# Two fp16 parts for the probabilities, second masks on TensorE, the projection a round later

## The reference, cut to what matters

```
def _layer(x, wqkv, qs, ksc, wo, lg, lb, w1, b1, w2, b2):
    h = shift_token(x)                         # second half of the columns from the row before
    q, k, v = split(h @ wqkv)                  # 8 heads of 64
    q, k = rotary_xpos(l2norm(q) * qs, l2norm(k) * ksc)
    # windows of 128: each query sees its own and the previous window,
    # masked to i >= j and i <= j + 128
    o = softmax(8 * q @ k.T, masked) @ v
    x = x + o @ wo
    h = layernorm(shift_token(x)) * lg + lb    # eps 1e-5
    a, g = split(h @ w1 + b1)                  # 682 columns each
    return x + (a * gelu(g)) @ w2 + b2
```

## Time and profile before

| | |
|---|---|
| median of three runs | 3973.07 us (3972.77 to 3973.07) |
| the profiled execution's own time | 3974.68 us |
| its span | 3972.9 us |
| mean granted clock of TensorE | 0.960 of its upper level |
| busy: TensorE, its weight loads | 3510.6 us, 2099.6 us |
| busy: VectorE, ScalarE, GpSimd | 2638.4, 2148.6, 1522.5 us |
| DMA | 139 MB, 35 GB/s in the mean |

### The profile page before, as it was taken

The page is one execution under the profiler, slowest core; times in us unless marked ns, Lnnn a source line. Parts: engine busy times, 40 slices in busy tenths (PEclk is TensorE's granted clock), DMA queues, the critical chain, the costliest instruction groups (busy, mean ns, idle before and its releaser), DMA issues.

```text
span 3972.9 us, 72434 instructions
## 1 busy us (share of the span) xinstructions
PE 3510.6 (88%) x26976; PEld 2099.6 (53%) x26976; DVE 2638.4 (66%) x4180; ACT 2148.6 (54%) x2585; POOL 1522.5 (38%) x1584
## 2 busy tenths in 40 slices
PE   2888888888866799999999999887999999999999
PEld 1223232323224566667666766555666766667666
DVE  4778777777744567666676666656677666776664
ACT  0566565656543356555555555443655556555554
POOL 1212121111114345455455554343455544455443
PEclk7999999999987899999999999998999999999999
DMA  2222222222120000010000101010000110001101
GB/s 56 48 60 54 58 55 57 56 56 57 45 82 6 14 21 19 18 34 19 21 18 18 34 19 42 20 50 19 27 24 24 34 35 25 24 27 31 37 19 35
DMA packets 149003, 139.02 MB, mean 35 GB/s; under 512 B 11132, under 2 KB 147376, under 8 KB 148912
## 3 DMA queue, kind: packets, MB, share of 16 engines
q1 hardware_dynamic: 148912, 137.78, 13.1%
HBM read 70.40 MB, written 33.55 MB: 26 GB/s over the span
## 4 chain that ended last, share of the span: by engine, by line
issue 29%; POOL 21%; PE 15%; DVE 4%; ACT 2%; POOLq 0%; DMA 0%; SPq 0%; DVEq 0%; ACTq 0%
POOL f_u L1478 7%; POOL f_u L1483 5%; PE f_p L1104 3%; PE f_p L1123 3%; POOL f_hT L1494 3%; POOL f_Pl L1502 2%; PE f_p L1145 2%; PE f_p L1023 2%; POOL f_xb L1511 2%; PE f_p L1086 2%; POOL f_Pl L1504 1%; POOL f_qst L1488 1%; PE f_p L1090 1%; POOL f_mark_l L1499 1%; DVE f_negm L1360 1%
## 5 line engine op out<-in xcount | busy, mean ns | idle before, releaser
L654 DVE TENSOR_REDUCE m_negm<-m_p 128x2 f16<-128x1024 f32 x512 | 608.3, 1221 | 170.4 <-PE m_p L473 168.5
L576 ACT ACTIVATE m_Pr<-m_p 128x1024 f32<-128x1024 f32 x512 | 500.6, 1020 | 163.9 <-PE m_p L492 159.4
L1478 POOL TENSOR_TENSOR f_u<-f_u,f_bt 128x1024 f32<-128x1024 f32 x128 | 301.9, 2358 | 561.2 <-DVE f_bt L1332 561.2
L1104 PE MATMUL f_p<-f_vl,f_Pl 128*128 128x65 f32 x3584 | 426.1, 279 | 30.7 <-POOL f_Pl L1504 30.7
L1104 PEld LDWEIGHTS f_p<-f_vl,f_Pl 128*128 128x128 f32 x3584 | 416.0, 195 | 41.0 <-POOL f_Pl L1504 31.4
L1229 ACT ACTIVATE f_Pl<-f_p 128x896 f32<-128x896 f32 x256 | 220.5, 914 | 328.8 <-PE f_p L1090 221.6
L1494 POOL TENSOR_TENSOR f_hT<-f_gates,f_hT 128x512 f16<-128x512 f32 x192 | 223.8, 1166 | 396.5 <-ACT f_gates L1252 395.1
L501 PE MATMUL m_o<-m_Pr,m_vm 128*32 128x512 f32 x2048 | 341.6, 645 | 13.0 <-ACT m_Pr L576 13.0
L1023 PE MATMUL f_p<-f_wq_h,f_xT_h 128*128 128x512 f16 x768 | 295.8, 385 | 62.4 <-DVE f_mark_x L1318 45.1
L1244 ACT ACTIVATE f_gates<-f_p,f_bias 128x512 f32<-128x512 f32 x192 | 131.4, 684 | 344.8 <-PE f_p L1145 344.7
L1360 DVE TENSOR_REDUCE f_negm<-f_p 128x4 bf16<-128x1024 f32 x256 | 295.7, 1222 | 15.0 <-PE f_p L1056 15.0
(11 more groups left out here) (219 smaller groups left out, 7533.7 us busy)
## 6 DMA issues: line engine op xcount, KB each, us to landing
f_xs<-out SPq DMA_DIRECT2D x32, 512.0 KB, 4.8
f_xr<-out SPq DMA_DIRECT2D x32, 512.0 KB, 4.6
out<-f_xb SPq DMA_DIRECT2D x32, 512.0 KB, 3.3
m_xin<-in_L_attn_x SPq DMA_DIRECT2D x16, 512.0 KB, 4.1
out<-m_xn SPq DMA_DIRECT2D x16, 512.0 KB, 3.0
m_QT<-m_hi SPq DMA_DIRECT2D x128, 64.0 KB
m_KT<-m_hi SPq DMA_DIRECT2D x128, 64.0 KB
m_xr<-in_L_attn_x SPq DMA_DIRECT2D x16, 512.0 KB, 4.8
```

What stands on the lines that cost most here:

```text
L576: act.activation(Pr[kt % 2][:, 2 * u:2 * u + 2, :].rearrange("p h t -> p (h t)"), psum[w.slot("M2", g, kt, u)][:, :], ACT.Exp).then_inc(*w ...
L654: dve.tensor_reduce(negm[:, t, pr // 2, :, pr % 2], psum[w.slot("M1", h, u)][:, :].rearrange("p (a k) -> p a k", a=2), AX.X, ALU.max, nega ...
L1104: mm = pe.matmul(psum[w.slot("PV", hp)][:, e * T + t * (DH + 1):e * T + (t + 1) * (DH + 1)], Pl[h % 4][:, at * W:(at + 1) * W], vl[:, j, h ...
L1478: pool.tensor_tensor(u[t][:], u[t][:], bt[:], ALU.add).then_inc(*bt_used.up(I))
```

## The change

- The probabilities are kept in two fp16 parts. ScalarE's exponentials go to one of two fp32 buffers; new steps make the high part (`C.PH`, ScalarE) and the low part (`C.PL`, VectorE) into four fp16 buffers. Values get a low part too (a step `C.V` on VectorE). `C.PV` has three fp16 matmuls where one fp32 matmul stood.
- The masks of the second scores are added in PSUM by matmuls with the identity; GpSimd's `affine_select` and marks go.
- `OT` and `WO` form a stage D that runs with N's element, i-2, a round later, early in the round. The loads and conversions of `wo` move with it (`WS` on SP, staged in the fp16 probability buffers).
- The keys' low parts (`SH`) go from VectorE to GpSimd. Of `LN`, the inverse root goes to GpSimd (`LR`, a power and one Newton step, as the first phase has it); VectorE keeps the statistics (`LN`) and the normalising (`LA`).
- The last block of `W1` packs gate and value into one weight tile of 64 + 42 columns (`wt_h`, `wt_l`).
- `hp_` has three buffers instead of two; in `L1` `start` is set for every second mask matmul. All five lists are written anew.

```diff
     order = {
-        "PE": """C.V,0 C.V,1 C.V,2 C.V,3 A.XT C.ST,0 A.QK,0 C.ST,1 A.QK,1 C.ST,2 A.QK,2 C.ST,3 A.QK,3 F.W1,0 F.W1,1 C.L1,0 C.L1,1
-               F.W1,2 C.L1,2 C.L1,3 F.W1,3 F.W1,4 F.W1,5 C.LM F.W2,0 C.L2,0 F.W2,1 F.W2,2 C.L2,1 C.PV,0 C.L2,2 C.L2,3 C.PV,1 C.PV,2
-               C.OT,0 C.PV,3 N.XH C.OT,1 C.WO,0 C.WO,1 C.WO,2 C.WO,3""",
...
+        "PE": """C.V,0 C.V,1 C.V,2 C.V,3 A.XT C.ST,0 D.OT,0 D.OT,1 A.QK,0 C.ST,1 A.QK,1 C.ST,2 A.QK,2 C.ST,3 A.QK,3 D.WO,0 C.L1,0
+               D.WO,1 D.WO,2 D.WO,3 C.L1,1 F.W1,0 C.L1,2 F.W1,1 C.L1,3 F.W1,2 F.W1,3 C.LM F.W1,4 F.W1,5 C.L2,0 F.W2,0 F.W2,1 C.L2,1
+               F.W2,2 C.L2,2 C.PV,0 C.L2,3 C.PV,1 N.XH C.PV,2 C.PV,3""",
+        "ACT": """C.V,0 C.V,1 C.V,2 C.V,3 A.XT C.ST,0 D.OT,0 D.OT,1 A.QK,0 C.ST,1 A.QK,1 C.ST,2 A.QK,2 C.ST,3 A.QK,3 F.W1,0 F.W1,1
+               F.H1,0 F.W1,2 F.H1,1 F.W1,3 C.LM F.H1,2 F.W1,4 F.H1,3 F.W1,5 F.H1,4 F.H1,5 C.L2,0 C.PH,0 A.HI,0 C.L2,1 C.PH,1 C.L2,2
+               C.PH,2 A.HI,1 C.L2,3 C.PH,3 N.XH A.HI,2 A.HI,3""",
+        "DVE": """C.V,0 C.V,1 C.V,2 C.V,3 A.XT D.OT,0 D.OT,1 A.QK,0 A.QK,1 A.QK,2 A.QK,3 D.WO,0 D.WO,1 D.WO,2 C.L1,0 D.WO,3 C.L1,1
+               F.W1,0 C.L1,2 F.W1,1 C.L1,3 C.LM F.W1,2 A.RN F.W1,3 F.W1,4 F.W1,5 F.ZB N.LN F.W2,0 C.PL,0 C.PL,1 F.W2,1 F.W2,2 N.LA
+               C.PL,2 C.PV,0 C.PL,3 C.PV,1 N.XH C.PV,2 C.PV,3""",
+        "POOL": """A.QK,0 A.QK,1 A.QK,2 A.QK,3 F.H1,0 F.H1,1 F.H1,2 F.H1,3 F.H1,4 F.H1,5 A.NM,0 N.LR A.SQ,0 A.SH,0 A.NM,1 A.SQ,1 A.SH,1
+               A.NM,2 A.SQ,2 A.SH,2 A.NM,3 A.SQ,3 A.SH,3 N.LS""",
+        "SP": """A.XT N.LX C.XR F.W2,0 F.W2,1 F.W2,2 N.XH""",
     }
...
-        r2 = weave(("third", layer), A=2, C=1, N=0)
+        r2 = weave(("third", layer), A=2, C=1, D=0, N=0)
...
-        Pall = sb("Pl", [P, 4, NK], F32)
-        Pl = [Pall[:, r, :] for r in range(4)]
+        Pl = [sb(f"Pl{r}", [P, NK], F32) for r in range(2)]
+        Pall = sb("Ph", [P, 4, 2, NK], F16)
+        Pp = [Pall[:, r] for r in range(4)]
...
@@ PE, l2
+                for e in range(2):
+                    for j in range(NT):
+                        pe.matmul(dst(e, j), identb[:], masks[:].rearrange("p a k -> p (a k)")[:, 0:min(2 * W, T - j * W)],
+                                  start=False, stop=False, skip_group_check=True)
...
@@ PE, pv
-                pe.wait_ge(*masked.at(I, 2 * (2 * hp + 2)))
+                pe.wait_ge(*p_lo_ready.at(I, 2 * hp + 2))
...
+                            pe.matmul(dst, p_hi, vl[:, j, h, 0:DH + 1], start=(t == 0), stop=False, skip_group_check=True)
+                            pe.matmul(dst[:, 0:DH], p_hi, vl[:, j, h, DH + 1:], start=False, stop=False, skip_group_check=True)
+                            mm = pe.matmul(dst, p_lo, vl[:, j, h, 0:DH + 1], start=False, stop=(j == t), skip_group_check=True)
...
@@ PE, w1_
+                if f == NF - 1:
+                    for c in range(NC):
+                        for k, (a_, b_) in enumerate(((wt_h, xhT_h), (wt_l, xhT_h), (wt_h, xhT_l))):
+                            mm = pe.matmul(psum[w.slot("W1", f)][0:HALF + TAIL, 0:T], a_[:, c, :], b_[:, c, :],
+                                           start=(c == 0 and k == 0), stop=(c == NC - 1 and k == 2))
...
@@ ACT
             def l2(I, hp):
+                for h in (2 * hp, 2 * hp + 1):
+                    act.wait_ge(*w.is_full("L2", h))
+                    if h >= 2:
+                        act.wait_ge(*p_lo_ready.at(I, h - 1))
+                    act.activation(Pl[h % 2][:], psum[w.slot("L2", h)][:, 0:NK], ACT.Exp, scale=1 / KBOOST)\
+                        .then_inc(*w.frees("L2", h))
+
+            def p_hi(I, hp):
                 if hp >= 2:
                     act.wait_ge(*w.is_full("PV", hp - 2))
                 for h in (2 * hp, 2 * hp + 1):
...
+                    act.wait_ge(*w.is_drained("L2", h))
+                    act.activation(Pp[h % 4][:, 0, :], Pl[h % 2][:], ACT.Copy).then_inc(*p_hi_ready.up(I))
...
@@ DVE
+            def v_(I, t):
+                dve.wait_ge(*v_hi_ready.at(I, t + 1))
+                dve.scalar_tensor_tensor(vl[:, t, :, DH + 1:], psum[w.slot("V", t)][:, 0:INNER].rearrange("p (h d) -> p h d", h=H),
+                                         1 / WSCALE, vl[:, t, :, 0:DH], ALU.mult, ALU.subtract).then_inc(*w.frees("V", t))
+
+            def p_lo(I, hp):
+                for h in (2 * hp, 2 * hp + 1):
+                    dve.wait_ge(*p_hi_ready.at(I, h + 1))
+                    dve.tensor_tensor(Pp[h % 4][:, 1, :], Pl[h % 2][:], Pp[h % 4][:, 0, :], ALU.subtract).then_inc(*p_lo_ready.up(I))
...
@@ POOL
+            def roots(link, v, y, t):
+
+                def factor(n):
+                    return factors[:, n:n + 1].to_broadcast([P, v.shape[1]])
+                link(pool.tensor_tensor(y, v, factor(1), ALU.pow))
+                link(pool.tensor_tensor(t, y, y, ALU.mult))
...
+            def sh(I, t):
+                pool.wait_ge(*hi_ready.at(I, t + 1))
+                pool.tensor_tensor(klt[t][:].rearrange("p (h d) -> p h d", h=H), u[t][:, INNER:].rearrange("p (h d) -> p h d", h=H),
+                                   khh[t][:, :, 0:DH], ALU.subtract).then_inc(*stack_ready.up(I))
...
@@ SP
+            def ws(I):
+                if I.b > 0:
+                    hold(on_ready.at(all_of_layer(I.b), 0))
+                load(I, wo_loaded, st_o, wo[I.b].rearrange("(c p) n -> p c n", p=P))
```

More of the change, by code:

```diff
@@ L805, in layers_phase @@
[L805 to L809, removed]
@@ L829, in layers_phase @@
     K = [Inst(f"K{layer}", 0, (lambda i, layer=layer: layer)) for layer in range(L)]
-    sections = [Section("queries", {engine: [("WQ", K[0])] for engine in ENGINES})]
+    sections = [Section("queries", {engine: [("WQ", K[0]), ("WS", K[0])] for engine in ENGINES})]
     for layer in range(L):
         more = layer > 0
-        r0 = weave(("first", layer), A=0, **(dict(N=-1, F=-2) if more else {}))
+        r0 = weave(("first", layer), A=0, **(dict(D=-1, N=-1, F=-2) if more else {}))
         r1 = weave(("second", layer), A=1, C=0, **(dict(F=-1) if more else {}))
-        r2 = weave(("third", layer), A=2, C=1, N=0)
[L836 to L839, removed]
+        r2 = weave(("third", layer), A=2, C=1, D=0, N=0)
+        for engine in ("ACT", "DVE"):
+            with_steps(r0, engine, "end" if more else "start", ("WO_", K[layer]))
+        with_steps(r1, "PE", "end", ("WO_", K[layer]))
         with_steps(r1, "SP", "end", ("WE", K[layer]))
@@ L1103, in pv @@
                             at = 2 * j + t - j
-                            mm = pe.matmul(psum[w.slot("PV", hp)][:, e * T + t * (DH + 1):e * T + (t + 1) * (DH + 1)],
-                                           Pl[h % 4][:, at * W:(at + 1) * W], vl[:, j, h, :], start=(t == 0), stop=(j == t),
-                                           skip_group_check=True)
+                            dst = psum[w.slot("PV", hp)][:, e * T + t * (DH + 1):e * T + (t + 1) * (DH + 1)]
+                            p_hi, p_lo = [Pp[h % 4][:, part, at * W:(at + 1) * W] for part in range(2)]
+                            pe.matmul(dst, p_hi, vl[:, j, h, 0:DH + 1], start=(t == 0), stop=False, skip_group_check=True)
+                            pe.matmul(dst[:, 0:DH], p_hi, vl[:, j, h, DH + 1:], start=False, stop=False, skip_group_check=True)
+                            mm = pe.matmul(dst, p_lo, vl[:, j, h, 0:DH + 1], start=False, stop=(j == t), skip_group_check=True)
                 mm.then_inc(*w.fills("PV", hp))
             def ot(I, half):
-                w.wait(w.is_drained("PV", 2 * half + 1), w.is_free("OT", half))
+                pe.wait_ge(*on_ready.at(I, half + 1))
+                pe.wait_ge(*w.is_free("OT", half))
                 for c in (2 * half, 2 * half + 1):
@@ L1180, in wf @@
                 act.wait_ge(*w1_scaled.at(I, NC))
+                for g, c0 in ((1, 0), (0, HALF)):
+                    act.activation(wt_h[:, :, c0:c0 + TAIL], st_1[:, :, hidden(g, NF - 1)], ACT.Copy)
                 act.activation(w1_h[:], st_1, ACT.Copy).then_inc(*w_hi.up(I))
             def xt(I):
-                act.wait_ge(*vl_ready.before(I, 1))
+                act.wait_ge(*v_hi_ready.before(I, 1))
                 act.wait_ge(*w.is_full("XT"))
@@ L1267, in _ @@
                 dve.memset(m[:, NF - 1, :], 0.0)
-            dve.memset(mark_a[:], 0.0)
+            for m in (wt_h, wt_l):
+                dve.memset(m[:].rearrange("p c n -> p (c n)"), 0.0)
             dve.memset(mark_v[:], 0.0).then_inc(const_done, 1)
@@ L1309, in wf @@
                 dve.wait_ge(*w_hi.at(I, 4))
+                for g, c0 in ((1, 0), (0, HALF)):
+                    dve.tensor_tensor(wt_l[:, :, c0:c0 + TAIL], st_1[:, :, hidden(g, NF - 1)], wt_h[:, :, c0:c0 + TAIL], ALU.subtract)
                 dve.tensor_tensor(w1_l[:], st_1, w1_h[:], ALU.subtract).then_inc(*w_lo.up(I))
@@ L1457, in _ @@
                 pool.memset(m[:], 0.0).then_inc(mask_zero, 1)
-            pool.wait_ge(mask_zero, len(mats))
```

(3 more changed lines are left out.)

119 lines of the change are left out of this document (57 added, 62 removed).

## The result

The changed kernel takes 3928.32 us (median, 3925.87 to 3928.82), the kernel before 3973.07: a ratio of 0.9884, 95% interval 0.9866 to 0.9901. It is faster, by 1.2%: 45 us where 73 were forecast. The profiled executions have spans of 3926.1 and 3972.9 us, a difference of 46.8.

What follows compares the result with a forecast made beforehand. TensorE's stream was taken as the bound, 78.8 us of matmuls and 3 of waits a round. From 3973 us, -53 in steady rounds and -23 in others gave 3897, stated as 3900, range 3830 to 3980.

Steps and rivals of the forecast that it cites:

- The main term: Steady rounds, 26 in the layers phase: from 81.87 to 79.8 us each, -2.05 x 26 = -53 us.
- the other rounds: First, second, third, late and last rounds and tails of the layers: together -23 us (-45 to +10).
- the 79 to 80.5: Sign that the forecast is right: marks of neighbouring steady rounds stand 79 to 80.5 us apart.
- rival 2: fp16 `C.PV` matmuls no cheaper than 56 ns: 4 us more stream, a round of 81.2, 3936 us; 14%.
- `C.PV`'s price: On TensorE, 168 fp16 matmuls a round at 0.032 us, 5.4 us instead of 12.6, saving 7.2.
- TensorE's stream: TensorE's matmuls in a steady round: from 78.8 to 73.4 us, -5.4 (-6.3 to -1.4).
- The other engines: Busy time a steady round: VectorE to 60 us, ScalarE to 54, GpSimd to 38; none the bound by its sum.
- The places of the new waits: TensorE newly waits before `C.PV,3`, `N.XH` and the first `C.V`; 2 to 3 us come back as waits.
- the term of the shared port: Round's end: GpSimd blocks two or three of eight `C.PL` on VectorE by about a microsecond each.
- the layout: Steady round laid out by engine lists and prices, one blocked `C.PL` in it; the round takes 79.8 us.
- Rival 1: The new order costs nothing: stream of 73.4 plus 3 us of waits, a round of 76.4, 3808 us; 13%.
- Rival 3: GpSimd's chain through `A.HI,3` and every `C.PL` blocked at the round's end: a round of 83.2, 3996 us; 15%.

Runs made afterwards that it cites:

- e4: Changed kernel with `C.PV` in fp32 again, without the fp16 high and low parts of probabilities or the low part of V: 4004.00 us.
- e11: Changed kernel with `A.NM,0` to `A.NM,2` moved earlier in GpSimd's list, `A.NM,3` left late behind `A.SH,2`: 3851.91 us.
- e10: Changed kernel with `A.RN` in three parts on VectorE, all `A.NM` between GpSimd's `F.H1`, and `A.HI,0` to `A.HI,2` earlier on ScalarE: 3875.72 us.
- e13: Changed kernel with `A.RN` in three parts on VectorE, the third ahead of `C.LM`, and all `A.NM` between GpSimd's `F.H1`; ScalarE's list unchanged: 3805.69 us.
- e6: Changed kernel without the mask matmuls in `C.L2`, exponentials at scale 0: 3927.92 us.
- e8: Changed kernel with the heads' inverse norms (`A.RN`) as a power and one Newton step on GpSimd, all `A.NM` behind it: 3962.39 us.
- e3: Changed kernel without low parts of the probabilities: `C.PL` writes one column instead of 896, `C.PV` takes the high part again: 3831.74 us.

## Why the prediction was right, and where it was off

**The direction was right, and so was its cause: a shorter stream of TensorE, of which waits at the round's end take most back. The main term was a third of its size: the steady round's gain was 0.76 us, not 2.05.** 26 times the difference is 33 us; the other rounds gave 4 us more than said, which leaves about the 28 us between 3900 and 3928. Of the 47 us that came, 20 are from the 26 steady rounds, where 53 were forecast, and 27 from the others, where 23 were. The marks lie 81.1 us apart, outside the 79 to 80.5 that were to show the forecast right.

In a round at a clock of 1.00, 80.8 us, the stream is 73.8 (73.4 said) and the waits 7.0 (6.4 said: 3, 2 to 3 and 0.9); the last 0.3 to 81.1 goes with a lower clock. The round alone would also have fitted rival 2's 81.2; `C.PV`'s price tells them apart.

**`C.PV`: right.** TensorE's timeline of one pair, the first two and the last of its 42 matmuls:

```profile
2960.97 0.20 PE L1113 MATMUL f_p<-f_vl,f_Ph 128*128 128x65 f16 x1
2961.01 0.20 PE L1114 MATMUL f_p<-f_vl,f_Ph 128*128 128x64 f16 x1
...
2962.23 0.19 PE L1115 MATMUL f_p<-f_vl,f_Ph 128*128 128x65 f16 x1
```

1.26 us over 41 steps is 0.031 us a matmul; 0.032 was said. Rival 2 falls. TensorE: Matmul & The Clock Gate in the Trainium skill (section Back-to-back issue gap) has about 81 ns at 128 columns in sustained streams. Taken over to 65 columns, as the prediction's estimate did, it is more than twice the trace's 31 ns.

- **TensorE's stream: right within 0.4.** 73.79 for 73.4; e4's 80.46 shows the other side.
- **The other engines.** ScalarE 52.96 for 54, VectorE 62.6 for 60, GpSimd 41.3 for 38. The blocked time, 3.8 us a round above the shortest `C.PL`, is more than what VectorE has above the sum; the sum without it was 1 us too high. GpSimd's excess is in the main `A.NM` and `A.SQ` held up (a mean of 2.33 and 1.41 for 1.90 and 1.29 of the earlier trace rows).
- **The places of the new waits: right.** `C.PV,3` 2.6 us, `C.L2,3` 1.5 (behind `F.W2`, as laid out), `N.XH` 0.9, the first `C.V` 0.6; ScalarE's V stands behind `A.HI,3`, which ends 4.3 us after `C.V,0` (4.7 said).
- **The step that failed is the term of the shared port.** "Two or three blocked by about a microsecond" were two, of 1.7 us each, and the price of the other side was missing: the `A.NM` that blocks is held up by 0.85 us as well, and with it `A.HI,2` behind it. In the layout only `C.PL,1` was blocked. `C.PL,3`, on which `C.PV,3` hangs, was not. The prediction had "If none were, 1 us a round would come back"; e11 shows that 2.5 to 2.7 come back from blocks moved out of the way alone (some 0.3 of it perhaps by the clock, 1.00 throughout e11's steady rounds). The layout without blocks, 79.8 less 1, was near: e11 has 78.6 and 78.4. GPSIMD Engine Reference in the Trainium skill (section Specifications), with a port shared for VectorE instructions of two SBUF inputs or in a 2-port mode, agrees with all of these rows of `C.PL` (two SBUF inputs, 2.78 us for 1.09). `N.LA` in e10 is a case of one SBUF tensor in: by that page it has to be the 2-port mode, which no row names.
- **A second, smaller term was not in the prediction:** the granted clock was 1.00 in all steady rounds before; in the changed kernel it is 0.98 in 9 of layer 1's 12 intervals. The three at 1.00 take 80.77 us in the mean, the nine 81.23, so my estimate is some 0.35 us a round, 9 us in the run; it is rough, since three of the nine take no longer than 80.9. In the nine it is 0.72 to 0.93 over the 3.5 us around the wait ahead of `C.PV,3` and back at 1.00 before the next mark. In layer 1 of e13, whose waits there are 0.9 us, all twelve are at 1.00; in its layer 0 one is at 0.98 and takes 77.8 us, the others 76.7.
- **The other rounds: -27 for -23, in part by luck** (the -46.8 less the -18 above, without the two steady rounds that are left in it): misses of several us in both directions cancel. Layer 0's second is -12.3 as said; the third rounds -10.5 and -9.1 where -4 was said, layer 1's second -1.1 for -6, its first -1.5 for +3, and what is behind the last mark is +7.4 with a steady round and a tail in it, for +2. Why each missed stays open.
- **Rival 1** (a round of 76.4, 3808 us) was not what this order gives. With GpSimd's and VectorE's lists changed, e13 reaches 3805.69. **Rival 3** named the port and the chain at once; the port was real, and dearer than in the forecast but cheaper than in this rival (2.5 to 2.7 us a round from e11, against 4.4 from 78.8 to 83.2), the chain through `A.HI,3` was worth nothing (e11).

## What to carry to other kernels

Where VectorE gets an instruction with two SBUF inputs near GpSimd work, lay the two engines' lists side by side and look at which pairs overlap: each overlap can cost nearly the full length of the other's instruction, on both engines (1.7 us of an `A.NM` of 1.9 on VectorE, 1.0 of a `C.PL` of 1.1 on GpSimd), and it costs the most just ahead of the step that the bound engine waits for. Moving three GpSimd instructions to another place was worth more (76 us) than the whole change (45). Once waits set the end of a round, removing work from the busiest engine need give nothing back: in e6 it returned as a longer wait and a lower clock.

## What the runs showed of the hardware

- A GpSimd power grows with its columns: 1.07 us for four, 10.53 for 64, where a product of 64 columns (L1515 of e8) takes 0.29.
- VectorE and GpSimd take turns by whole instructions: 1.09 + 1.90 + 1.09 us of work took 3.96, and both sides wait. A VectorE `TENSOR_SCALAR` with one fp32 SBUF tensor in (0.34 us) is held up as well, to 1.20.
- fp16 pairs of weight load and matmul with 64 or 65 columns start 0.031 us apart, though each load lasts 0.10 us; the records of fp32 ones with 65 columns 0.113.
- What a lower granted clock costs depends on what waits behind it: in e3 neighbouring rounds at 1.00 and at 0.98 both take 77.93 us; in e4, where TensorE's stream sets the round, 82.77 and 84.38.
